# Who adds the causal mask to the last query tile's scores before their maximum is taken

## What is computed

```
q = (x @ q_w + q_b).reshape(B, T, 16, 8).transpose(0, 2, 1, 3)
att = einsum('bhqd,bhkd->bhqk', q, k) / sqrt(8)
att = att + slope[h] * (key - query)
att = where(key <= query, att, -inf)
att = softmax(att, axis=-1)
y = einsum('bhqk,bhkd->bhqd', att, v)
```

## Time and profile before

| what | value |
|---|---|
| median of 3 runs | 1090.53 us (1090.3 to 1091.83) |
| the profiled execution's span, first to last instruction | 1172.6 us; nothing outside it is recorded |
| PE, DVE, ACT, POOL busy | 1049.2, 761.8, 738.6, 634.6 us |
| attention stage, first scores to last mask matmul | 60.9 to 600.7 us |
| line 603, both forms | 1280 matmuls, 162.1 us busy, 212 ns mean |
| line 916, reductions of 512 columns | 640, 681 ns |

### The profile page before, as it was taken

One profiled execution on the slowest core, in us unless ns is written; L12 is line 12 of the kernel. 1 busy time (PEld: TensorE's weight loads), 2 busy tenths in 40 slices (PEclk: granted clock), 3 DMA queues, 4 the chain that ended last, 5 costly groups with the idle time before them and its releaser, 6 DMA issues. The chain is left out here.

```text
span 1172.6 us, 27905 instructions
## 1 busy us (share of the span) xinstructions
PE 1049.2 (89%) x9236; PEld 724.0 (62%) x9236; DVE 761.8 (65%) x1861; ACT 738.6 (63%) x1630; POOL 634.6 (54%) x1133
## 2 busy tenths in 40 slices
PE   3999999999999989999997898766879999899993
PEld 1445455555455435454543787666769999899882
DVE  3888888888888888888951484221213334566596
ACT  1167887778777667778786344433336777677653
POOL 1045545545455448778877256655654444455542
PEclk9789999999999989999999899878779999999997
DMA  5233233243333314343321511111212223344343
GB/s 139 68 90 100 77 85 90 76 109 86 84 82 78 107 54 112 94 131 89 93 62 49 216 36 47 59 56 57 60 54 61 64 54 87 88 122 120 113 132 94
DMA packets 123243, 101.84 MB, mean 87 GB/s; under 512 B 18736, under 2 KB 113846, under 8 KB 122450
## 3 DMA queue, kind: packets, MB, share of 16 engines
q1 hardware_dynamic: 113362, 78.18, 25.1%
q0 software_dynamic: 8640, 16.87, 4.5%
q10 hardware_dynamic: 1104, 5.01, 1.1%
HBM read 39.31 MB, written 35.66 MB: 64 GB/s over the span
## 5 line engine op out<-in xcount | busy, mean ns | idle before, releaser
L711 ACT ACTIVATE probs<-scores 128x512 f32<-128x512 f32 x640 | 355.4, 603 | 78.3 <-PE scores L620 73.7
L779 POOL TENSOR_SCALAR_AFFINE_SELECT probs<-probs 128x256 f32<-128x256 f32 (+1 forms) x640 | 223.8, 364 | 180.1 <-ACT probs L711 168.2
L1213 DVE TENSOR_TENSOR e_hid<-e_gate,e_up_ps 128x352 f32<-128x352 f32 (+2 forms) x190 | 106.5, 560 | 259.9 <-ACT e_gate L1488 161.1
L916 DVE TENSOR_REDUCE rowmax<-maxed 128x1 f32<-128x512 f32 (+1 forms) x384 | 246.2, 682 | 33.6 <-PE maxed L603 30.2
L597 PE MATMUL maxed<-kstack,qstack 64*128 64x512 bf16 (+3 forms) x1024 | 232.3, 315 | 15.8 <-DMA kstack<-parts 8.5
L620 PE MATMUL scores<-qstack,kstack 64*128 64x512 bf16 (+3 forms) x1024 | 229.2, 303 | 7.2 <-ACT probs L711 6.2
L1571 POOL DMA_INDIRECT y_tokens<-e_raw,e_row_i x142 | 140.2, 987 | 147.7 <-ACT e_raw L1510 116.1
L636 PE MATMUL pv<-probs,vaug 128*32 128x512 f32 (+3 forms) x2048 | 192.7, 449 | 0.4 <-POOL probs L779 0.4
L916 DVE TENSOR_REDUCE maxB<-maxed 128x4 f32<-128x512 f32 x256 | 165.3, 681 | 20.6 <-PE maxed L603 18.6
L620 PEld LDWEIGHTS scores<-qstack,kstack 64*128 64x128 bf16 x1024 | 68.9, 94 | 160.9 <-ACT probs L711 103.9
L603 PE MATMUL maxed<-causal,halves 64*128 64x128 bf16 (+1 forms) x1280 | 162.1, 212 | 0.0
(11 more groups left out here) (185 smaller groups left out, 1568.5 us busy)
## 6 DMA issues: line engine op xcount, KB each, us to landing
qstack<-parts SPq DMA_DIRECT2D x96, 128.0 KB
kstack<-parts SPq DMA_DIRECT2D x96, 128.0 KB
x_sorted<-zeros SPq DMA_DIRECT2D x16, 580.5 KB
e_xs<-x_sorted SPq DMA_DIRECT2D x142, 64.5 KB
e_raw<-y_tokens SPq DMA_DIRECT2D x64, 128.0 KB
xin<-in_x SPq DMA_DIRECT2D x16, 256.0 KB, 3.2
e_group_in<-x1T_all SPq DMA_DIRECT2D x16, 256.0 KB, 3.0
out<-e_raw SPq DMA_DIRECT2D x64, 64.0 KB
```

The costliest lines, as they stand in the source:

```text
L711: act.activation(probs[g % 2][:, u * T:(u + 1) * T], scores[st.at(0, SEQ_UNITS, UNITS * g + u) % SB][:], ACT.Exp).then_inc(S["exp_done"], 1)
L779: pool.affine_select(out=view, in_=view, compare_op=ALU.is_ge, fill=0.0, base=0, pattern=pattern, channel_multiplier=-1).then_inc(S["maske ...
L916: dve.tensor_reduce(out, keys, AX.X, ALU.max).then_inc(S["max_taken"], 1)
L1213: dve.tensor_tensor(hid[step % len(hid)][rows, 0:cols], gate[step % 2][rows, 0:cols], up_ps[step % 2][rows, 0:cols], ALU.mult).then_inc(S[ ...
```

## The change

For banks of kind 0 PE no longer adds the mask of the diagonal blocks. The product itself is now the only matmul of such a bank and releases DVE. A new constant `last_mask`, 128 by 512 in float32 (256 KB, loaded on ACT's queue at the start), is -1e38 above the diagonal of the last 128 columns and 0 elsewhere. DVE's `tensor_tensor_reduce` reads the bank from PSUM and `last_mask` from SBUF, adds them, writes the sum as bf16 to one of two scratch tiles `summed` that nobody reads, and gives the maximum over the row to `rowmax`. It waits in addition for the bank two before, which wrote the same scratch tile. The banks of the other two kinds are as before.

```diff
--- before.py
+++ after.py
@@ -95,7 +95,9 @@
     row, col = np.arange(P)[:, None] % ROWS, np.arange(P)[None, :]
     half = np.stack([col == row, col == row + ROWS], axis=1).astype(np.float32)
     later = np.where(col[:, 0:CUT] > row, NEG, 0).astype(np.float32)
-    return bf16_bits(half), bf16_bits(np.stack([later, later], axis=1))
+    last = np.zeros((P, T), np.float32)
+    last[:, T - P:] = np.where(col > np.arange(P)[:, None], NEG, 0)
+    return bf16_bits(half), bf16_bits(np.stack([later, later], axis=1)), last
 
 
 def max_stage(n):
@@ -166,7 +168,7 @@
     return [(h, 1, 0), (h + 2, 1, 2 * P)]
 
 
-DIAGONAL = (slice(3, 4), slice(0, 4, 3), slice(1, 4, 2))
+DIAGONAL = (None, slice(0, 4, 3), slice(1, 4, 2))
 MAX_AT = (10, 20, 30, 0)
 PLACES = {
     "PE": {0: "xt", 1: "pv0", 3: "q", 4: "pv1", 6: "pv2", 7: "k", 8: "pv3", 10: "y0", 12: "pv0 y1", 13: "pv1", 14: "pv2",
@@ -361,6 +363,8 @@
         ident = keep["ident"]
         halves = sb("halves", [P, 2, P], BF16)
         causal = sb("causal", [P, 2, CUT], BF16)
+        last_mask = sb("last_mask", [P, T])
+        summed = [sb(f"summed{n}", [P, T], BF16) for n in range(2)]
         zeros = sb("zeros", [P, RW])
         wkv_in = sb("wkv_in", [P, 2 * C])
         wq = sb("wq", [P, C])
@@ -581,7 +585,7 @@
                     off = max_stage(n)
                     if n == 0:
                         if st.first(off):
-                            pe.wait_ge(S["masks_loaded"], 48)
+                            pe.wait_ge(S["masks_loaded"], 64)
                         if st.number + off < STACKS:
                             pe.wait_ge(S[f"stack_rows_loaded{st.stack(off)}"], STACK_ROWS_IN)
                         pe.wait_ge(stack_loaded[st.stack(off)], st.loaded(off))
@@ -591,6 +595,11 @@
                     bank = maxed[st.at(off, MAXB, n) % MB]
                     q, ks = qstack[st.stack(off)], kstack[st.stack(off)]
                     blocks, kind = max_blocks(n), n % 10 // QUAD
+                    if kind == 0:
+                        h, i, col = blocks[0]
+                        rows, slot = rows_of(h, ROWS)
+                        pe.matmul(bank[:], q[rows, slot, i * P:], ks[rows, slot, :], start=True, stop=True).then_inc(S["max_ready"], 1)
+                        return
                     first = True
                     for h, i, col in blocks:
                         rows, slot = rows_of(h, ROWS)
@@ -600,7 +609,7 @@
                     rows = rows_of(blocks[0][0], ROWS)[0]
                     diagonal = bank[:].rearrange("p (j c t) -> p j c t", c=P // CUT, t=CUT)[:, DIAGONAL[kind]]
                     for half in range(P // CUT):
-                        done = pe.matmul(diagonal[:, :, half, :], halves[rows, half, :], causal[rows, 0:1 if kind == 0 else 2, :],
+                        done = pe.matmul(diagonal[:, :, half, :], halves[rows, half, :], causal[rows, :, :],
                                          start=False, stop=half == 1, skip_group_check=True)
                     done.then_inc(S["max_ready"], 1)
 
@@ -723,6 +732,7 @@
 
                 act.dma_start(halves[:].bitcast(U16), io["halves"]).then_inc(S["masks_loaded"], 16)
                 act.dma_start(causal[:].bitcast(U16), io["causal"]).then_inc(S["masks_loaded"], 16)
+                act.dma_start(last_mask[:], io["last_mask"]).then_inc(S["masks_loaded"], 16)
                 act.dma_start(vb[:], io["kv_b"][C:2 * C].unsqueeze(0).to_broadcast([P, C])).then_inc(S["masks_loaded"], 16)
                 act.wait_ge(S["const_loaded"], CONSTS)
                 act.activation(qb_scaled[:], qb[:], ACT.Copy, scale=SCALE).then_inc(S["const_ready"], 1)
@@ -832,7 +842,7 @@
                     elif name == "v":
                         dve.wait_ge(S["v_ps"], st.at(1, 1, 1))
                         if st.first(1):
-                            dve.wait_ge(S["masks_loaded"], 48)
+                            dve.wait_ge(S["masks_loaded"], 64)
                         if st.every or st.number + 1 >= 2:
 
                             dve.wait_ge(S["pv_ready"], st.at(-1, 4, 4))
@@ -908,8 +920,12 @@
                             dve.wait_ge(S["m_ps"], st.at(0, 1, 1))
                     bank = maxed[st.at(max_stage(n), MAXB, n) % MB][:]
                     if n % 10 < QUAD:
-                        out, keys = best[:, h, 3:4], bank.unsqueeze(1)
-                    elif n % 10 < 2 * QUAD:
+                        if n >= 2 or not st.first(max_stage(n)):
+                            dve.wait_ge(S["max_taken"], st.at(max_stage(n), MAXB, n - 1))
+                        dve.tensor_tensor_reduce(out=summed[n % 2][:], in0=bank, in1=last_mask[:], scale=1.0, scalar=NEG, op0=ALU.add,
+                                                 op1=ALU.max, accum_out=best[:, h, 3:4]).then_inc(S["max_taken"], 1)
+                        return
+                    if n % 10 < 2 * QUAD:
                         out, keys = maxB[:, h, :, :].rearrange("p a b -> p (a b)")[:, QT - 2:], bank.rearrange("p (j t) -> p j t", t=P)
                     else:
                         out, keys = best[:, h:h + 2, 1], bank.rearrange("p (j t) -> p j t", t=2 * P)
@@ -1616,8 +1632,8 @@
     q, k = stack_constants()
     before, rank, slot_row, ids = routing_constants()
     eye = np.eye(P, dtype=np.float32)
-    halves, causal = causal_constants()
-    return {"ident": eye, "halves": halves, "causal": causal, "qstack_rows": q,
+    halves, causal, last_mask = causal_constants()
+    return {"ident": eye, "halves": halves, "causal": causal, "last_mask": last_mask, "qstack_rows": q,
             "kstack_rows": k, "before": before, "rank": rank, "slot_row": slot_row, "ids": ids}
```

## The result

The changed kernel takes 1083.38 us in the median (1079.95 to 1085.71, 7 runs) against 1090.53 (1088.38 to 1095.66, 7 runs) for the kernel before: a ratio of 0.9931, with a 95% interval from 0.9911 to 0.9951. It is faster, by 5.3 to 9.7 us. The forecast was 1087.8, faster, with a range from 1083 to 1101: the sign and the range hold, but the gain is more than twice the 2.7 us of the sum.

A forecast was written before the change was run, and what follows sets the result against it. The prediction took PE, in a chain with ACT, as the bound, with DVE close behind. A PE gain of 4.3 us less 1.6 us lost at the start gave -2.7 us from 1090.53: 1087.8 us, range 1083 to 1101.

The forecast's parts named there:

- What bounds the kernel: Attention stage: PE fullest, 35.4 of 36 us, in a chain swinging between PE and ACT; DVE close behind at 31.4.
- The gain on PE: Five and a half mask pairs on the path at 0.057 us: 0.31 us a step, 4.3 us over 14 steps.
- The price on DVE: Sum with maximum plus a small instruction: 0.07 to 0.37 us more a bank, 0.08 taken, 1.3 us a step.
- Where DVE would be tight: Three changed banks, then residual sum and statistics, before PE's bank at 336.77: DVE 0.18 us late, covered by ACT's backlog.
- The start: Before the first scores, 20 changed banks at 0.08 us without cover: 1.6 us lost, no PE gain there.
- The mask's transfer: Load of the 256 KB mask at the start: hidden; with no cover it would cost about 3 us.
- The sum: Whole kernel: -4.3 + 1.6 = -2.7 us, carried over to the median of 1090.53 as 1087.8 us.
- swallowed: Rival: a shorter PE stretch only lengthens its wait for ACT, so only the start counts: 1092.1 us; chance 0.15.
- DVE is not the bound: Judges the rival that changed banks delay later releases and PE stops at them: +10.4 us, so 1101; chance 0.19.
- Half rate: Rival: DVE's sum runs at one column in two cycles, 8.3 us more a step: 1173 us; chance 0.05.
- The small instruction's waiting for the large one's end: Rival: on DVE a bank then costs 0.16 us, the start loses 3.2: 1090.4 us; chance 0.17.
- All pairs on the path: Rival: every mask pair on PE counts, 0.91 us a step, 11.2 us less in all: 1079 us; chance 0.07.

The follow-up runs named there:

- the fourth group: Changed kernel, but PE keeps its mask matmuls in banks 0 to 3 of the next sequence and DVE adds the mask too: 1084.66 us.
- the first group: Changed kernel, but PE keeps its mask matmuls in banks 10 to 13 of the step and DVE adds the mask too: 1090.03 us.
- the second profile of before: The kernel before, with no edit, run and profiled once more: 1090.55 us, span 1088.8.
- the PE side alone: Against the kernel before, the masks leave PE and DVE keeps the plain maximum, so the last query tile's maximum is unmasked: 1083.38 us, ratio 0.995.
- the DVE side alone: Against the kernel before, DVE takes the masked maximum while PE still adds its masks: 1091.13 us, ratio 1.0013.

## Why the prediction was right, and where it was not

- **What bounds the kernel: right.** Masks off PE alone give the whole gain of a step, the DVE edit alone gives none, and a step of all masks on DVE is shorter still, so DVE does not set the step. That it is PE together with ACT fits the fourth group, whose pairs are worth nothing, and ACT's shorter wait.
- **The gain on PE: right in kind, a little small.** 0.31 us a step forecast, 0.34 to 0.37 measured. The groups were forecast at 0.11, 0.11, 0.09 and 0, and measured at 0.12 to 0.16, 0.11 to 0.12, 0.10 and 0. In the first group more pairs count than I had, those at 310.40 and beside the scores at 312.51 too, while a pair is worth 0.04 and not 0.057. Two errors of opposite sign left the sum nearly right, and that was luck.
- **The price on DVE: the step that failed.** "A bank then costs DVE 0.07 to 0.37 us more, and I take 0.08": it is 0.01, below the low end. I took that end from four tiny aggregations in a row, 0.07 from start to start. But a small instruction *behind a large one* starts when the next large one could, and that one starts with it. The nearest row had the right instruction size and the wrong neighbour. The large instruction's own 0.01 was right. Where DVE would be tight was right too: PE's new wait of 0.15 us is at that place, and no step is longer for it.
- **The start: the loss forecast is not there, and one that was put at nothing is.** The mask's transfer was called hidden. But PE's first matmul, which waits for an input tile, starts at 6.3 us in both profiles of before and at 6.8 to 7.5 in all eleven profiles of kernels that load the mask; the max pass's first product comes at 23.1 in the former and at 23.6 to 24.4 in the latter. So 0.5 to 1.3 us seem to go there. That the transfer itself holds up the tile was not tried, and every kernel with an edit loads it. With 0.01 a bank the 20 banks cost 0.2 us and not 1.6. From one profile to the next the first scores moved from 59.4 to 62.4 us over all kernels, and the two profiles of before differ by 1.5 (60.9 and 59.4), the changed kernel's by as much (59.7 and 61.2). A loss of 1.6 can't be excluded from those rows; the pair's 0.61 us excludes it. What the masks gone from PE gave at the start, if anything, is not resolved. DVE's first long wait there did get shorter, 1.40 to 0.82 us near 34.5, though in the second profile of before it was 1.22.
- **The sum.** With the two sizes put right it reads -14 x 0.36 + 0.2 = -4.8 us, against -2.7, and the late start would take it to about -4. The intervals of the changed kernel (-5.3 to -9.7, and -3.5 to -8.6 when run once more) and of the PE side alone (-2.7 to -8.3) have -5.3 to -8.3 in common, whose near end is 0.5 to 1.3 us off. The rest, 2 to 3 us in the medians, is not settled, but part of it goes with the mean granted clock that is listed with the timed runs. Of the kernel before, 15 runs at 0.970 have a median of 1091.34 us and ten at 0.973 one of 1087.71; of the changed kernel, five at 0.970 have 1085.15, six at 0.972 have 1083.42 and three at 0.975 have 1081.49. Straight lines of one slope through all runs of both that have a clock listed put the difference at equal clock at some 5.5 us, an estimate, give or take 0.8. That the changed kernel's runs had the higher clock a little more often would make up the rest of its median, and whether the change brought that about is open. In the profiles the largest other difference is the step with the routing: 46.9 us in both of before, 44.0 and 43.6 in the changed kernel's. It goes in part with the granted clock, as the next section shows. But with the DVE side alone it was 44.4, and that kernel's median did not fall.
- **The rivals.** The gain is not swallowed: ACT's wait for PE shrank and PE's wait for ACT did not grow. DVE is not the bound at 31.8 us: PE's waits for its maxima did appear, but the kernel without them has the same step. Half rate has fallen: 685 ns for 512 columns. The small instruction's waiting for the large one's end has fallen as well: it starts 0.61 us after a start, while the large one lasts 0.685, and the next large one starts together with it. The Trainium skill's VectorE: DVE Perf Modes, in "The DRAIN you can't avoid", has the next operation wait for an empty pipe unless it is not held; by the model in its "Two Vector instructions with no wait between them" the pair here is not held, and the trace agrees with that model, for the accumulator read too. All pairs on the path would have been 0.91 us a step; with the fourth group at nothing, that is excluded.

## What to carry to other kernels

Short work that is only a correction (a mask, a bias) is cheap to move off the engine that sets the step into an instruction that another engine runs anyway, if that engine has room. Price such an instruction by the distance between starts of its neighbours, not by its duration, and beside a neighbour of the size that it will have. When the total is uncertain by 0.2%, count steps: eight steps by one recurring event repeated to 0.1 us from one profile to another of the same kernel, and keeping one group at a time split a gain of 0.36 us a step into parts that add up. Look at the first microseconds too before a transfer is called hidden.

## What the runs showed of the hardware

- DVE's read of its accumulator lasts 83 ns, and with it the large instruction costs 0.01 us more than a reduction; a one-column memset behind it, 59 ns long, costs another 0.01. Both overlap the start of the next large instruction.
- The sum with maximum runs at the reduction's rate, with one source in PSUM and one in SBUF: 685 ns for 512 columns with the next start after 0.61; 0.55 and 0.48 for 384, 0.29 and 0.21 for 128.
- A pair of short mask matmuls was worth 0.04 us on PE in the piece that was followed, though the trace gives each a mean of 0.189.
- The step with the routing goes in part with the granted clock. The stretch from 380 to 450 us around it, in the second profile of before:

```profile
380.00:450.00 70.00, 63.45 (x641) 31.69 (x641) 61.54 (x132) 46.89 (x91) 36.93 (x80) 0.93 0.33 90
```

and in the second one of the changed kernel:

```profile
380.00:450.00 70.00, 63.00 (x632) 29.49 (x629) 64.85 (x173) 48.83 (x96) 40.31 (x88) 0.98 0.31 83
```

PE is idle for 6.5 and 7.0 us in it, in both a pause of nearly 5 us, and then runs for some microseconds at a mean of 0.5 to 0.6, so mostly at 1.2 GHz. Over all profiles, at a mean of 0.93 the step took 45.0 to 46.9 us (seven), at 0.95 it took 43.7 to 44.4 (four), at 0.98 it took 43.6 and 43.7. Both profiles of before were at 0.93 and both of the changed kernel above it, but the PE side alone was at 0.93 and the DVE side alone at 0.95, so this follows neither half of the change. Nor is the clock all of it: at the same 0.93 the step took 46.9 in both profiles of before and 45.0 with the PE side alone.
- With all masks on DVE the granted clock fell to 0.95 over two of eight steps that do the same work, with PE busy for 97% of each, and these two were 1.2 us longer. What brought it on was not tried; without it that kernel would be faster still.
